# Latent attention layers: where the value product, the scores and the projections stand in TensorE's order

## What is computed

```python
h = concatenate([x, latents], axis=1)             # 256 rows a sample
q = (latents @ q_w + q_b).reshape(b, k_len, NH, DH)          # NH 16, DH 32
kv = (h @ kv_w + kv_b).reshape(b, p + k_len, NH, DH, 2)
kmat, v = (kv[..., 0], kv[..., 1])
attn = einsum('bkhd,bnhd->bhkn', q, kmat) / DH
attn = softmax(where(full_mask, attn, -inf))
attn_out = einsum('bhkn,bnhd->bkhd', attn, v).reshape(b, k_len, H)
attn_out = attn_out @ out_w + out_b + residual
out = rmsnorm(attn_out, postnorm_w)
out = gelu(out @ mlp_w1 + mlp_b1) @ mlp_w2 + mlp_b2
return out + residual
```

## Time and profile before

| | |
|---|---|
| median of 3 runs | 2555.6 us |
| the runs | 2562.81, 2555.38, 2555.6 us |
| the profiled execution | 2562.53 us |
| its span | 2560.7 us |
| busy PE, DVE, ACT, POOL | 96%, 48%, 42%, 44% |
| mean granted clock of TensorE | 0.982 |
| latent layer 0 with its first block | from 0 to about 438 us |
| latent layer 3 | from about 1772 to 2204 us |

### The profile page before, as it was taken

How to read it: one execution, slowest core, us unless ns; L and a number is a source line. 1 busy time by engine, 2 the same in 40 slices (tenths; PEclk the granted TensorE clock), 3 DMA queues, 4 the chain that set the end, 5 groups by cost and what they waited for, 6 DMA issues and landing times.

```text
span 2560.7 us, 48767 instructions
## 1 busy us (share of the span) xinstructions
PE 2452.8 (96%) x18464; PEld 2053.4 (80%) x18464; DVE 1231.4 (48%) x3296; ACT 1085.6 (42%) x3712; POOL 1120.2 (44%) x1972
## 2 busy tenths in 40 slices
PE   7999998999999999998888999999999999899999
PEld 6888886888888878886777788888888888788887
DVE  4555655332224667766666332243455556432332
ACT  4555554111114787777767111111455555311111
POOL 2453545600053787778876630033344443730000
PEclk9999999999999999998988999999999999999999
DMA  4111312211033233223443320122021111320100
GB/s 162 59 59 59 104 55 79 83 50 50 1 109 126 74 106 121 96 97 125 150 161 121 115 91 1 50 87 74 26 88 63 51 43 61 114 87 1 50 33 17
DMA packets 106774, 198.07 MB, mean 77 GB/s; under 512 B 8304, under 2 KB 35632, under 8 KB 103600
## 3 DMA queue, kind: packets, MB, share of 16 engines
q1 hardware_dynamic: 106544, 194.97, 23.1%
HBM read 136.22 MB, written 58.72 MB: 76 GB/s over the span
## 4 chain that ended last, share of the span: by engine, by line
PE 79%; ACT 11%; DVE 5%; POOL 3%; issue 1%; DMA 1%; SPq 0%; DVEq 0%; POOLq 0%
PE banks L326 70%; ACT plain_high L731 5%; PE banks L467 5%; PE banks L497 3%; ACT plain_low L731 2%; POOL plain_high L1342 2%; ACT plain_work L796 1%; DVE stats L1134 1%; PE banks L521 1%; ACT plain_work L715 1%; DVE plain_work L1149 0%; DMA plain_high<-attention_w 0%; DVE plain_high L1004 0%; ACT plain_low L715 0%; DVE rounded_low L1053 0%
## 5 line engine op out<-in xcount | busy, mean ns | idle before, releaser
L326 PE MATMUL banks<-rounded_work,rounded_low 128*128 128x512 f32 (+1 forms) x2688 | 534.3, 355 | 11.5 <-DVE rounded_low L1166 9.5
L326 PEld LDWEIGHTS banks<-rounded_work,rounded_low 128*128 128x128 f32 x2688 | 445.3, 198 | 76.8 <-issue 15.9
L982 ACT ACTIVATE plain_work<-banks,columns 128x512 f32<-128x512 f32 x192 | 132.4, 690 | 870.8 <-PE banks L326 870.8
L326 PE MATMUL banks<-rounded_work,rounded_high 128*128 128x512 f32 (+1 forms) x2400 | 483.4, 355 | 2.1 <-DMA rounded_work<-ctx_split 1.7
L326 PEld LDWEIGHTS banks<-rounded_work,rounded_high 128*128 128x128 f32 x2400 | 396.6, 191 | 68.2 <-issue 6.2
L1342 POOL TENSOR_SCALAR plain_high<-plain_high,inv_sum 128x128 f32<-128x128 f32 (+1 forms) x768 | 296.6, 409 | 317.5 <-DVE inv_sum L1026 317.2
L1318 DVE CAST rounded_work<-plain_work 128x512 fp32r<-128x512 f32 x192 | 105.3, 549 | 685.7 <-ACT plain_work L982 674.9
L326 PE MATMUL banks<-rounded_low,rounded_work 128*128 128x512 f32 x1728 | 414.9, 391 | 0.0
L326 PE MATMUL banks<-rounded_high,rounded_work 128*128 128x512 f32 (+1 forms) x1728 | 390.2, 377 | 0.0
L326 PEld LDWEIGHTS banks<-rounded_low,rounded_work 128*128 128x128 f32 x1728 | 321.6, 188 | 68.6 <-issue 2.8
L326 PEld LDWEIGHTS banks<-rounded_high,rounded_work 128*128 128x128 f32 x1728 | 309.1, 188 | 60.5 <-issue 1.4
(11 more groups left out here) (106 smaller groups left out, 3120.9 us busy)
## 6 DMA issues: line engine op xcount, KB each, us to landing
plain_work<-x SPq DMA_DIRECT2D x96, 256.0 KB, 3.2
plain_work<-mlp_w SPq DMA_DIRECT2D x96, 256.0 KB, 2.7
rounded_work<-ctx_split SPq DMA_DIRECT2D x16, 1024.0 KB, 6.0
u<-plain_work SPq DMA_DIRECT2D x48, 256.0 KB, 2.8
plain_work<-u SPq DMA_DIRECT2D x12, 1024.0 KB, 7.2
x<-plain_work SPq DMA_DIRECT2D x48, 256.0 KB, 2.3
plain_work<-attention_w SPq DMA_DIRECT2D x44, 256.0 KB, 2.6
ctx_split<-rounded_work SPq DMA_DIRECT2D x8, 1024.0 KB, 5.6
```

Source lines behind the costliest of these rows:

```text
L326: mm = pe.matmul(dst, lhs(i), rhs(j), start=first and n == 0, stop=last and n == 2, skip_group_check=True)
L982: act.activation(gelu[:, j % 2, :], bank(key), ACT.Gelu_apprx_tanh, bias=col(y, 28 + j)).then_inc(evac_of(key), 1)
```

## The change

In both latent layers the value product of a round now stands directly ahead of the next round's scores, the transposes come behind these, and then three projections in a row. The value product of round 3 goes behind the last projections of the pair, so that it stands at the head of the next pair. The output projection of sample 2p-2 moves from the end of pair p-1 to round 1 of pair p, that of sample 2p-1 from round 1 to round 2. The orders of ScalarE, VectorE and GpSimd follow; `sp_latent` is unchanged.

```diff
--- before.py
+++ after.py
@@ -548,45 +548,49 @@
                 pe_values(pe, y, 0, i)
             for p in range(PAIRS):
                 more = p + 1 < PAIRS
+                if p:
+                    pe_attend(pe, y, p - 1, 3)
                 pe_scores(pe, y, p, 1)
                 pe_turn_probs(pe, y, p, 0)
                 if more and y.n:
                     pe_turn_x(pe, y, p + 1)
                 if p:
-                    pe_out(pe, y, 2 * p - 1)
-                pe_attend(pe, y, p, 0)
+                    pe_out(pe, y, 2 * p - 2)
                 if more:
                     pe_keys(pe, y, p + 1, 0)
                     pe_keys(pe, y, p + 1, 1)
-                pe_scores(pe, y, p, 2)
-                pe_turn_probs(pe, y, p, 1)
-                if more:
-                    pe_queries(pe, y, p + 1, 0)
                 else:
                     pe_turn_u(pe, M[y.n], 0, 0)
                     pe_turn_u(pe, M[y.n], 0, 1)
+                pe_attend(pe, y, p, 0)
+                pe_scores(pe, y, p, 2)
+                pe_turn_probs(pe, y, p, 1)
+                if p:
+                    pe_out(pe, y, 2 * p - 1)
+                if more:
+                    pe_queries(pe, y, p + 1, 0)
+                    pe_values(pe, y, p + 1, 0)
                 pe_attend(pe, y, p, 1)
-                if more:
-                    pe_values(pe, y, p + 1, 0)
-                    pe_values(pe, y, p + 1, 1)
                 pe_scores(pe, y, p, 3)
                 pe_turn_probs(pe, y, p, 2)
                 if more:
+                    pe_values(pe, y, p + 1, 1)
                     pe_keys(pe, y, p + 1, 2)
+                    pe_keys(pe, y, p + 1, 3)
                 else:
                     pe_turn_u(pe, M[y.n], 0, 2)
                     pe_turn_u(pe, M[y.n], 0, 3)
                 pe_attend(pe, y, p, 2)
                 if more:
-                    pe_keys(pe, y, p + 1, 3)
                     pe_scores(pe, y, p + 1, 0)
+                else:
+                    pe_out(pe, y, B - 2)
                 pe_turn_probs(pe, y, p, 3)
-                pe_out(pe, y, 2 * p)
-                pe_attend(pe, y, p, 3)
                 if more:
                     pe_queries(pe, y, p + 1, 1)
                     pe_values(pe, y, p + 1, 2)
                     pe_values(pe, y, p + 1, 3)
+            pe_attend(pe, y, PAIRS - 1, 3)
             pe_out(pe, y, B - 1)
 
         def pe_gqa(pe, y):
@@ -872,36 +876,36 @@
                     elif more:
                         act_stage(act, p + 1)
 
+                if p:
+                    act_heads(act, y, p - 1, 3)
                 act_round(act, y, p, 1, (p, 0), inputs)
-                act_heads(act, y, p, 0)
                 if more:
                     act_keys(act, y, p + 1, 0)
                     act_keys(act, y, p + 1, 1)
-                act_round(act, y, p, 2, (p, 1), nothing)
-                if more:
-                    act_queries(act, y, p + 1, 0)
                 else:
                     act_turn_u(act, M[y.n], 0, 0)
                     act_turn_u(act, M[y.n], 0, 1)
+                act_heads(act, y, p, 0)
+                act_round(act, y, p, 2, (p, 1), nothing)
+                if more:
+                    act_queries(act, y, p + 1, 0)
+                    act_values(act, y, p + 1, 0)
                 act_heads(act, y, p, 1)
-                if more:
-                    act_values(act, y, p + 1, 0)
                 act_round(act, y, p, 3, (p, 2), nothing)
                 if more:
                     act_keys(act, y, p + 1, 2)
+                    act_keys(act, y, p + 1, 3)
                 else:
                     act_turn_u(act, M[y.n], 0, 2)
                     act_turn_u(act, M[y.n], 0, 3)
                 act_heads(act, y, p, 2)
-                if more:
-                    act_keys(act, y, p + 1, 3)
                 if not more:
                     act_warm(act, 1 if y.n == 0 else 5, ACT.Gelu_apprx_tanh)
                 act_round(act, y, p + 1, 0 if more else None, (p, 3), nothing)
-                act_heads(act, y, p, 3)
                 if more:
                     act_queries(act, y, p + 1, 1)
                     act_values(act, y, p + 1, 2)
+            act_heads(act, y, PAIRS - 1, 3)
 
         def act_gqa(act, y):
             act_keys(act, y, 0, 0)
@@ -1188,37 +1192,40 @@
                     elif more:
                         dve_stage(dve, p + 1)
 
+                if p:
+                    dve_heads(dve, y, p - 1, 3)
                 dve_round(dve, y, p, 1, (p, 0), inputs)
                 if p:
-                    dve_out(dve, y, 2 * p - 1)
-                dve_heads(dve, y, p, 0)
+                    dve_out(dve, y, 2 * p - 2)
                 if more:
                     dve_keys(dve, y, p + 1, 0)
                     dve_keys(dve, y, p + 1, 1)
-                dve_round(dve, y, p, 2, (p, 1), nothing)
-                if more:
-                    dve_queries(dve, y, p + 1, 0)
                 else:
                     dve_turn_u(dve, M[y.n], 0, 0)
                     dve_turn_u(dve, M[y.n], 0, 1)
+                dve_heads(dve, y, p, 0)
+                dve_round(dve, y, p, 2, (p, 1), nothing)
+                if p:
+                    dve_out(dve, y, 2 * p - 1)
+                if more:
+                    dve_queries(dve, y, p + 1, 0)
+                    dve_mask(dve, y, p + 1)
                 dve_heads(dve, y, p, 1)
-                if more:
-                    dve_mask(dve, y, p + 1)
+                dve_round(dve, y, p, 3, (p, 2), nothing)
+                if more:
                     dve_values(dve, y, p + 1, 1)
-                dve_round(dve, y, p, 3, (p, 2), nothing)
-                if more:
                     dve_keys(dve, y, p + 1, 2)
+                    dve_keys(dve, y, p + 1, 3)
                 else:
                     dve_turn_u(dve, M[y.n], 0, 2)
                     dve_turn_u(dve, M[y.n], 0, 3)
                 dve_heads(dve, y, p, 2)
-                if more:
-                    dve_keys(dve, y, p + 1, 3)
+                if not more:
+                    dve_out(dve, y, B - 2)
                 dve_round(dve, y, p + 1, 0 if more else None, (p, 3), nothing)
-                dve_out(dve, y, 2 * p)
-                dve_heads(dve, y, p, 3)
                 if more:
                     dve_queries(dve, y, p + 1, 1)
+            dve_heads(dve, y, PAIRS - 1, 3)
             dve_out(dve, y, B - 1)
 
         def dve_gqa(dve, y):
@@ -1401,10 +1408,12 @@
                 more = p + 1 < PAIRS
                 pool_norm(pool, y, p, 1)
                 if p:
+                    pool_root(pool, y, 2 * p - 2)
+                pool_norm(pool, y, p, 2)
+                if p:
                     pool_root(pool, y, 2 * p - 1)
                 if not more:
                     pool_mlp_tiles(pool, y, 8, 10)
-                pool_norm(pool, y, p, 2)
                 pool_bias(pool, y, 2 * p)
                 if 1 <= p <= 4:
                     pool_mlp_tiles(pool, y, 2 * p - 2, 2 * p - 1)
@@ -1418,7 +1427,7 @@
                     pool_norm(pool, y, p + 1, 0)
                 else:
                     pool_mlp_tiles(pool, y, 12, 14)
-                pool_root(pool, y, 2 * p)
+            pool_root(pool, y, B - 2)
             pool_root(pool, y, B - 1)
             pool_mlp_tiles(pool, y, 14, 32)
 
```

8 lines of the change are left out of this document (4 added, 4 removed).

## The result

The changed kernel takes **2566.3 us** (median of 6 runs, 2565.5 to 2572.5). The kernel before takes 2555.5 in the 6 runs beside it (2554.5 to 2562.8). The ratio is 1.004, with a 95% interval of 1.0026 to 1.0055: 10.8 us slower, where +3.3 was forecast. 2566.3 lies within the range of 2548 to 2572, which is wide, but 7 us above the 2559 of the forecast and above the 2563 from which the prediction called a time slower.

What follows compares the result with a forecast made beforehand. TensorE's own stream was taken to bound the latent layers' steady part, GpSimd's probabilities the last pair. Terms +3.1 - 4.2 + 1.0 - 0.6 + 4.0 sum to +3.3 us, giving 2559 us from a median of 2555.6; range 2548 to 2572.

Steps and rivals of the forecast that it cites:

- Part 1: Middle pairs: value product directly followed by scores saves 0.70 us per pair of 1.50 spent on going between groups.
- Part 2: Layer 0, six pair periods: the next pair's first key projection waits 1.51 us instead of 0.30; +3.1 us in all.
- Rival C: Layer 0: no wait before the next pair's keys, as input rounding starts sooner; 2550 us, chance 0.10.
- rival A: Layer 0: the new 1.51 us wait lowers the clock, two key projections run at half speed; +17, 2576 us, chance 0.12.
- Parts 3 and 4: Layer 3's six periods keep their 0.70 us gain with no new wait, -4.2 us; first pairs of both layers, +1.0 us.
- Part 4: First pair, both latent layers: value product formerly hidden in a wait comes after the keys, less boundary savings; +1.0 us.
- Part 5: Last pairs: one more output projection, GpSimd's normalisation 3 at +30.3 us after the first transposes; -0.3 a layer, -0.6 for two.
- Part 6: Last pairs: clock falls behind TensorE's 7 us idle ahead of the last transposes; 2.0 us a layer, +4.0 in all.
- Rival B: Last pairs: final transposes and value product don't restore the clock, 5.8 a layer instead of 2.0; 2566 to 2567, chance 0.18.
- Rival D: Both latent layers: all 1.50 us per pair of group-change cost goes, plus part of Rival C; 2545 us, chance 0.10.

Runs made afterwards that it cites:

- run 1: Changed kernel with every middle-pair value product one projection earlier, so a projection stands between it and the next scores; 2579.4 us, ratio 1.0084.
- Run 3: Changed kernel with both output projections ahead of the next pair's first key projection, the second key projection moved to the next group; 2555.3 us, ratio 0.9992.
- a_again: The changed kernel profiled again, with no edit; 2571.7 us.
- run 4: Changed kernel with 12, 5 and 6 matmuls of unused result put in three TensorE waits of each last pair; 2561.8 us, ratio 1.0017.
- run 10: Changed kernel with Run 3's edit, GpSimd's tiles 8 to 11 moved, and sample 14's output projection between last transposes and value product; 2536.9 us, ratio 0.9923.

## Why the prediction was right or wrong

- **Part 1, right.** In layer 3, where no wait was opened, a pair gave 50.86 - 50.19 = 0.67 for a forecast of 0.70 (0.62 and 0.70 over five pairs of each execution). That A and S cost nothing together and a projection between them does is run 1: 0.22 each time, with no wait in it. The Trainium skill, TensorEngine Tiling (Array Packing), section Tiling Modes, has each change of mode drain the engine; read as one equal price for each of four changes in a round it gave 0.38 a pair, and the 0.67 measured is not that.
- **Part 2, right.** K0 at T0 + 5.96 for 5.95, waited 1.51 as forecast; the pair 50.45 for 50.57. Run 3 takes the wait away and 1.49 us of the pair with it. Rival C fell on this, and rival A too: the granted clock of the middle pairs stays up behind the wait (1.00 from 99 to 109 us).
- **Parts 3 and 4, partly.** The middle pairs of layer 3 gave -0.67 each, but the stretch gave -4.6 instead of -6.4. In the first pair of layer 3, K0 now waits 2.83 us, and K0 and K1 take 7.05 us instead of 5.72 behind it:

```profile
1817.98 7.05 PE L326 MATMUL banks<-rounded_work,rounded_high 128*128 128x512 f32 x24 [2.83 <-DVE rounded_work L1107]
```

  From S1 to S2 of that pair it is 14.71 us, and 16.19 in `a_again`, where all three executions of the kernel before have 12.36 to 12.38: +3.1 in the mean. Part 4 charged a moved A0 and no clock there, 0.5 a layer.
- **Part 5, the size right, the picture not.** Normalisation 3 at +31.0 for +30.3, T3 at 429.39 - 397.27 = +32.1 for +31.4. But "TensorE is there at about +24.5" failed: it waits for VectorE at the MLP's input tiles (`pe_turn_u`), at A2 and at O14 and comes only with O14's end at about 426.2, +29. Since T3 waited for GpSimd anyway, this cost nothing at T3; it is the wait of 2.43 ahead of O14 behind which the clock fell first.
- **Part 6, the step that failed.** It says "I take 2.0 a layer". From T3 to the MLP's start the changed kernel takes 442.46 - 429.39 = 13.1 us, where 8.9 and 0.7 were forecast at full clock: 3.5 over, and run 4 gives some 3 us a layer back by keeping TensorE busy. I took the low third of the bounds because T2 in the kernel before had brought the clock back within its own length. Here T3 (3.81), A3 (1.94) and O15 (4.87) all ran slow, with waits of 1.20 and 1.43 between them. One recovery behind a wait is no measure for a place with a wait ahead of each group. Layer 3 of the kernel before, which is not among the rows, has a slower one: A1 takes 1.94 us at 2178.29, and the granted clock is 0.67 from 2178 to 2188. Together the parts come to this: of the 7.5 us by which 10.8 exceeds the forecast, 3.7 lie in the two last pairs (T3 0.7 late and 1.5 more clock behind it, in the profiled execution), 1.8 in layer 3 ahead of its last pair, 0.3 in the two stretches that the executions don't resolve, and 1.7 in the base.
- **The base.** The base is the time to which the sum is added. The profile I argued from had a mean clock of 0.982, where the runs of the kernel before have a median of 0.985; the changed kernel's was typical of its runs. Profile against profile the change costs 4.0 us, median against median 10.8, stretch by stretch over five executions 9.1. I noted the 7 us between executions, and did not ask whether the change would lower the mean clock of all of them. Of the six runs of the changed kernel none came under 2565.5. That more waits mean more half clock fits the mean clocks and run 4; what gives one execution a better clock than another stays open.
- **Rival B** had the right place, and I gave it 0.18. That its time came out is luck: it charged 5.8 a layer behind T3, where 3.5 were lost, and the rest of the 2566 lay in layer 3 and in the base. Its reason was that transposes do not bring the clock back; the Trainium skill, TensorE: Matmul & The Clock Gate, Part 4: PE-mode transpose, has the full clock not engage for them. The traces speak against it for these transposes. Timeline of PE in run 10, layer 3, T3 and O14:

```profile
2166.00 3.65 PE L467 MATMUL banks<-ident,plain_low 128*128 128x128 f32 x16
2169.57 2.99 PE L326 MATMUL banks<-rounded_high,rounded_low 128*128 128x512 f32 x12
```

  The granted clock was 0.55 from 2166.00 to 2169.50 and 1.00 from 2169.60 on. In layer 3 of `a_again` T3 ran at 0.58 and A3, 1.20 us of idle time behind it, in 1.08 us at 1.00. But in the profiled execution of the changed kernel (T3 3.81 us) the clock did not come back behind T3, nor behind A3, and what makes the difference stays open. Rival D fell on the 0.67 of Part 1.

## What to carry to other kernels

When an edit moves work past another engine's queue, price the ends of the loop first: twelve middle pairs gained or lost about 0.7 us each at most, two last pairs lost over 6 each, and two of the three repairs (moving four splits of tiles on GpSimd, and O14 back to its place) were made there. A wait on TensorE costs its length, as the 1.51 ahead of K0 did, and where the clock falls behind it, also what the lower clock takes from the groups that follow. In the last pairs, with several waits close together, that second part was some 3 us a layer; fill such waits with work that is due anyway, as O14 behind T3. And place the profiled execution among the other runs by its mean clock before adding a sum to it.

## What the runs showed of the hardware

- A projection of 12 wide matmuls between a value product and the scores took 2.94 us, 0.22 more than among projections (run 1); the value product followed directly by the scores took 1.01, as elsewhere.
- The time of one kernel's executions differs by 10 us (2562.4 to 2552.4) with the mean granted clock between 0.982 and 0.987, about 2 us for each 0.001.
- 23 matmuls a layer without use made the kernel 4.5 us faster, with GpSimd's normalisation 3 as late as before (30.8 us behind T0 for 31.0): O15 took 2.98 instead of 4.87 at the full clock.
- 16 transposes that began at half clock were followed by the full clock in some places (run 10, layer 3; the kernel before, layer 0) and by half clock in another (the changed kernel, layer 0).
